# A two-image Metaformer on one core: the second expert layer of image 0 taken tile by tile between pieces of image 1's convolution and routing, and image 0's chain to its slots taken between the steps of the dense layer

## What is computed

```python
x = x + _L0_conv_ref(_ln_c(x), ...)                 # window attention, 8 heads
t = t + _L0_ffn_ref(_ln_t(t), ...)                  # 8 experts, all computed for all tokens, weighted ("dense")
x = x + _L1_conv_ref(_ln_c(x), ...)                 # 1x1 conv, group norm, 9x9 + channel conv, group norm, 1x1 conv, group norm
t = t + _L1_ffn_ref(_ln_t(t), ...)                  # 16 experts, top 2 of each token
# _L1_ffn_ref:
probs = jax.nn.softmax(logits, axis=-1)
top_probs, top_idx = jax.lax.top_k(probs, 2)
hidden = jax.nn.silu(h1) * h2
expert_out = jnp.einsum('bseh,eho->bseo', hidden, w3)
return jnp.einsum('bseo,bse->bso', expert_out, dispatch)
```

## Time and profile before

| | us |
|---|---|
| median of 3 runs | 745.42 |
| lowest and highest | 742.21, 749.3 |
| profiled execution, device time | 743.35 |
| its span (first to last instruction) | 741.5 |
| PE, POOL, ACT, DVE busy in it | 556.7, 390.7, 356.0, 353.1 |
| mean granted TensorE clock (1 is 2.4 GHz) | 0.87 |

### The profile page before, as it was taken

How to read it: one execution, slowest core, us unless ns; L and a number is a source line. 1 busy time by engine, 2 the same in 40 slices (tenths; PEclk the granted TensorE clock), 3 DMA queues, 4 the chain that set the end, 5 groups by cost and what they waited for, 6 DMA issues and landing times.

```text
span 741.5 us, 16105 instructions
## 1 busy us (share of the span) xinstructions
PE 556.7 (75%) x5352; PEld 460.7 (62%) x5353; DVE 353.1 (48%) x1021; ACT 356.0 (48%) x860; POOL 390.7 (53%) x445
## 2 busy tenths in 40 slices
PE   0567889768799998999995798452699989999000
PEld 0456677657477776677762575242699989998000
DVE  4766877756302601300117435736555545555521
ACT  1578788985573448622246241340355545555000
POOL 4667799763373986843333000675674017720773
PEclk9969999999897999999976798555699999999555
DMA  9324322211453633321940000112144334542431
GB/s 341 90 62 114 91 77 80 68 55 45 163 190 138 214 140 124 118 96 42 289 122 1 0 1 0 39 51 67 57 137 136 98 87 124 140 120 60 129 84 53
DMA packets 82188, 74.98 MB, mean 101 GB/s; under 512 B 9102, under 2 KB 74854, under 8 KB 81742
## 3 DMA queue, kind: packets, MB, share of 16 engines
q1 hardware_dynamic: 77518, 64.72, 27.3%
q0 software_dynamic: 4608, 9.45, 4.6%
HBM read 50.92 MB, written 23.63 MB: 101 GB/s over the span
## 4 chain that ended last, share of the span: by engine, by line
PE 56%; ACT 12%; DVE 12%; POOL 8%; issue 8%; DMA 3%; SPq 0%; POOLq 0%; DVEq 0%; ACTq 0%
PE bank L797 12%; PE bank L759 8%; PE bank L858 8%; PE bank L742 7%; PE bank L808 6%; POOL gathered_or_att L636 4%; ACT normed L903 3%; PE bank L719 3%; PE bank L311 3%; ACT gathered_or_att L935 2%; DVE ln_stats L1078 2%; PE bank L788 2%; PE bank L757 1%; POOL gathered_or_att L577 1%; PE bank L692 1%
## 5 line engine op out<-in xcount | busy, mean ns | idle before, releaser
L612 POOL TENSOR_TENSOR padded_or_w<-padded_or_w,gathered_or_att 128x384 f32<-128x384 f32 x96 | 95.2, 999 | 87.4 <-ACT padded_or_w L974 71.9
L624 POOL DMA_INDIRECT sorted_x<-normed,slot x72 | 71.1, 988 | 97.3 <-DVE slot L1294 76.0
L636 POOL DMA_INDIRECT gathered_or_att<-sorted_y,slot x72 | 70.2, 975 | 94.4 <-DMA sorted_y<-padded_or_w 73.1
L974 ACT ACTIVATE padded_or_w<-bank,moe_b 128x384 f32<-128x384 f32 x96 | 55.3, 580 | 99.1 <-PE bank L742 98.8
L759 PEld LDWEIGHTS bank<-moe_or_conv,padded_or_w 128*128 128x128 f32 x576 | 82.4, 201 | 31.6 <-issue 10.6
L759 PE MATMUL bank<-moe_or_conv,padded_or_w 128*128 128x128 f32 x576 | 86.1, 289 | 0.0
L742 PE MATMUL bank<-chan_major,moe_or_conv 128*128 128x384 f32 x192 | 80.5, 503 | 0.2 <-ACT padded_or_w L974 0.2
L1323 DVE TENSOR_TENSOR att_or_moe<-att_or_moe,bank 128x256 f32<-128x256 f32 x104 | 43.7, 420 | 57.8 <-PE bank L808 40.9
L988 ACT ACTIVATE att_or_moe<-bank 128x256 f32<-128x256 f32 x104 | 39.9, 383 | 61.0 <-PE bank L797 59.8
L808 PE MATMUL bank<-w,att_or_moe 128*128 x416 | 63.7, 277 | 0.6 <-ACT padded_or_w L993 0.6
L797 PE MATMUL bank<-att_or_moe,chan_major 128*128 128x128 f32 x416 | 56.7, 281 | 6.9 <-DVE chan_major L1315 6.9
(11 more groups left out here) (168 smaller groups left out, 1081.9 us busy)
## 6 DMA issues: line engine op xcount, KB each, us to landing
gathered_or_att<-combine SPq DMA_DIRECT2D x24, 768.0 KB, 4.2
padded_or_w<-windows SPq DMA_DIRECT2D x192, 48.0 KB, 1.9
sorted_x<-zeros SPq DMA_DIRECT2D x26, 256.0 KB, 3.9
padded_or_w<-sorted_x SPq DMA_DIRECT2D x26, 256.0 KB
sorted_y<-padded_or_w SPq DMA_DIRECT2D x26, 256.0 KB, 2.3
padded_or_w<-in_moe_w SPq DMA_DIRECT2D x8, 512.0 KB, 5.3
residual<-in_x_tok SPq DMA_DIRECT2D x2, 1152.0 KB, 6.2
out<-residual SPq DMA_DIRECT2D x12, 192.0 KB, 2.4
```

The source lines that it names most:

```text
L612: nc.gpsimd.tensor_tensor(HB[n % DRING], HB[n % DRING], GB_[k % 3][:, n % 4, :], ALU.mult).then_inc(S("gated"), 1)
L624: nc.gpsimd.indirect_dma_start(xs_dram[b], bass.IndirectOffsetOnAxis(ap=POS[b][:, k, t:t + 1], axis=0), TN[b][:, t, :], None).then_inc(S(f ...
L636: nc.gpsimd.indirect_dma_start(G[k][:, t, :], None, ys_dram[b], bass.IndirectOffsetOnAxis(ap=POS[b][:, k, t:t + 1], axis=0)).then_inc(S(f" ...
L974: nc.scalar.activation(HB[n % DRING], banks[HBANK[n % 2]][:, 0:DG], ACT.Gelu, bias=B1C[:, e:e + 1]).then_inc(S("gelu"), 1)
```

## The change

- The second half of the dense layer (`D` 52 to 99) carries more: the taps of image 0 come in 6 pieces of 9 and no longer in 18 of 3, and all of image 0's chain up to the third piece of its choice (`XU`, group norm, `XUH`, `XZ`, layer norm, `RT`, `LG`, `RC 0` to `RC 3`) stands between steps.
- After the dense layer come image 1's layer norm, the rest of image 0's choice, `RP 0` and `RS 0` (slots and scatter), and only then image 1's first convolution, its taps and its middle group norm.
- `M 0` is no longer a loop but 56 written-out steps (`tile_steps`), and the rest of image 1's convolution, its routing, `RP 1` and `RS 1` stand between its steps 0 to 25. `M 1` stays a loop.
- PSUM banks: `M 0` has one bank for transposes and one for results where it had two of each; `XU` of image 1 has two where it had four.
- A group norm's DVE part is cut in three pieces (`GN`, `GV`, `GF`), so that other work can stand between.

```diff
-            *every(56, 2, groups("AN", "XL", 0)), (61, ("XC", 0)), (62, ("XCE", 0)), (62, ("GN", "XC", 0)), (65, ("GS", "XC", 0)), (67, ("GQ", "XC", 0)),
-            (69, ("XCH", 0)), *every(71, 1, taps(0, 0, 54)), (89, ("GN", "XM", 0)), (91, ("GS", "XM", 0)), (93, ("GQ", "XM", 0)), (95, ("XMH", 0)),
-            *every(96, 1, [("XU", 0, n) for n in range(4)])])
-        order += [*normed("XL", 1), *[("XU", 0, n) for n in range(4, 8)], ("GN", "XU", 0), *groups("XG", 1), ("GS", "XU", 0), ("GQ", "XU", 0),
-                  ("XC", 1), ("XCE", 1), ("GN", "XC", 1), ("GS", "XC", 1), ("GQ", "XC", 1), ("XCH", 1), *groups("XUH", 0),
...
+            *every(55, 1, groups("AN", "XL", 0)), (60, ("XC", 0)), (60, ("XCE", 0)), (60, ("GN", "XC", 0)), (62, ("GS", "XC", 0)), (62, ("GV", "XC", 0)), (64, ("GQ", "XC", 0)), (64, ("GF", "XC", 0)),
+            (65, ("XCH", 0)), *every(67, 1, taps(0, 0, 54, 9)), (73, ("GN", "XM", 0)), (75, ("GS", "XM", 0)), (75, ("GV", "XM", 0)), (76, ("GQ", "XM", 0)), (76, ("GF", "XM", 0)), (77, ("XMH", 0)),
+            *every(78, 0.25, [("XU", 0, n) for n in range(8)]), (80, ("GN", "XU", 0)), (82, ("GS", "XU", 0)), (82, ("GV", "XU", 0)), (83, ("GQ", "XU", 0)), (83, ("GF", "XU", 0)),
+            *every(83, 0.5, groups("XUH", 0)), *every(84, 0.5, groups("XZ", 0)), (87, ("LN", "LR", 1, 0)), (87, ("SQ", "LR", 1, 0)), (88, ("LV", "LR", 1, 0)),
+            *every(89, 0.5, groups("LT", "LR", 1, 0)), *every(90, 0.7, groups("RT", 1, 0)), (95, ("LG", 1, 0)), (96, ("RC", 1, 0, 0)), (96, ("RE", 1, 0)),
+            *every(98, 0.5, choice(1, 0, 1, 4))])
+        order += [("LN", "XL", 1), ("SQ", "XL", 1), ("LV", "XL", 1), *groups("LT", "XL", 1), *choice(1, 0, 4, 6), ("RP", 0), *groups("AN", "XL", 1),
+                  *groups("XG", 1), ("RS", 0), ("XC", 1), ("XCE", 1), ("GN", "XC", 1), ("GS", "XC", 1), ("GV", "XC", 1), ("GQ", "XC", 1), ("GF", "XC", 1), ("XCH", 1), *taps(1, 0, 54, 9),
+                  ("GN", "XM", 1), ("GS", "XM", 1), ("GV", "XM", 1), ("GQ", "XM", 1), ("GF", "XM", 1), ("XMH", 1)]
+        order += beside("M0", 0, J + MLAG, [
+            *every(0, 0.5, [("XU", 1, n) for n in range(8)]), (3, ("GN", "XU", 1)), (6, ("GS", "XU", 1)), (6, ("GV", "XU", 1)), (6, ("GQ", "XU", 1)), (6, ("GF", "XU", 1)),
+            *every(7, 0.5, groups("XUH", 1)), *every(8, 0.5, groups("XZ", 1)), (11, ("LN", "LR", 1, 1)), (11, ("SQ", "LR", 1, 1)), (12, ("LV", "LR", 1, 1)),
+            *every(12, 0.5, groups("LT", "LR", 1, 1)), *every(13, 0.5, groups("RT", 1, 1)), (16, ("LG", 1, 1)), (17, ("RC", 1, 1, 0)), (17, ("RE", 1, 1)),
+            *every(19, 1, choice(1, 1, 1, 6)), (24, ("RP", 1)), (25, ("RS", 1))])
+        order += [("M1",), *[("F", b) for b in range(NB)]]
...
-        UP = ((6, 7), (4, 5, 3, 2))
+        UP = ((6, 7), (4, 5))
+        PREFIX = ((6, 7), (4, 5))
+        XBANK, MBANK, OBANK = ((7, 7), (0, 1)), (2, 3), ((6, 6), (6, 7))
...
+        def tile_steps(eng, b, step, experts=True):
...
+            def at(j):
+                q, r = divmod(j, RING)
...
+                step(j, r, q % 2, expert, load)
+
+            return at
...
-                tile_groups(pe, b, step, 4)
+                return tile_steps(pe, b, step) if b == 0 else tile_groups(pe, b, step, MLAG)
```

More of the change, by code:

```diff
@@ L46, in metaformer_program @@
     DLAG, DRING = 4, 5
+    MLAG = 4
     ROWS = EX[0] * TG
@@ L186, in every, with taps @@
             return [(start + int(k * step), piece) for k, piece in enumerate(pieces)]
-        def taps(b, first, last):
-            return [("XT", b, m, min(m + 3, last)) for m in range(first, last, 3)]
+        def taps(b, first, last, size=3):
+            return [("XT", b, m, min(m + size, last)) for m in range(first, last, size)]
         def normed(*ln):
@@ L340, in run, with load, expert @@
                     phases[name](*where)
+        def tile_steps(eng, b, step, experts=True):
+            words, word = EPK[b], {}
+            def at(j):
+                q, r = divmod(j, RING)
+                if r == 0:
+                    word["before"] = word.get("now")
+                def load():
+                    if experts and q < J // RING:
+                        word["now"] = eng.value_load(words[0:1, q:q + 1], min_val=0, max_val=2 ** (BITS * RING) - 1)
+                def expert(k):
+                    slot = r - k
+                    bits = word["now"] if slot >= 0 else word["before"]
+                    shift = BITS * (slot % RING)
+                    return (bits >> shift) & (EX[1] - 1) if shift else bits & (EX[1] - 1)
+                step(j, r, q % 2, expert, load)
+            return at
         def tile_groups(eng, b, step, lag, experts=True):
@@ L813, in step @@
                     ok = lambda k: not isinstance(j, int) or 0 <= j - k < J
+                    if isinstance(j, int) and j == 0:
+                        ready()
                     if ok(0):
@@ L981, in xt @@
                         act.wait_ge(S("h_full1"), j + 1 - RING + b * J)
-                    nc.scalar.activation(XTS[r][:, :], banks[r % 2][:, 0:P], ACT.Copy).then_inc(S("xt_out"), 1)
+                    nc.scalar.activation(XTS[r][:, :], banks[XBANK[b][r % 2]][:, 0:P], ACT.Copy).then_inc(S("xt_out"), 1)
                 def nonlin(j, r):
@@ L1002, in step @@
                         tail(j - 4, r, 1 - h)
-                tile_groups(act, b, step, 4, experts=False)
+                return tile_steps(act, b, step, experts=False) if b == 0 else tile_groups(act, b, step, MLAG, experts=False)
             def gn_sqrt(name, b):
@@ L1332, in step, with ready @@
                         first(j - 2, (r + 2) % RING)
-                if b == 0:
-                    dve.wait_ge(S("moe1_in"), 16 * (1 + EX[1] // 2))
-                dve.wait_ge(S(f"experts{b}"), 1)
-                tile_groups(dve, b, step, 4)
+                def ready():
+                    if b == 0:
+                        dve.wait_ge(S("moe1_in"), 16 * (1 + EX[1] // 2))
+                    dve.wait_ge(S(f"experts{b}"), 1)
+                return tile_steps(dve, b, step) if b == 0 else tile_groups(dve, b, step, MLAG)
             def combine(b):
```

80 lines of the change are left out of this document (45 added, 35 removed).

## The result

The changed kernel takes 787.7 us (median of four runs, 781.6 to 793.8) against 746.6 for the kernel before: the ratio is 1.052, with a 95% interval of 1.047 to 1.058. That is slower by 5.2%. Ratios and intervals leave out executions in which the granted clock was lower and the time longer (here the one of 793.8), so that they can differ a little from the quotient of the medians. The profiled execution took 786.2 us, with a span of 784.3.

What follows compares the result with a forecast made beforehand. The prediction saw PE idle between two busy stretches; afterwards image 1's slots (587) and scatter bound `M 1`'s start at 637.5. Adding 134.4 and 1 gave span 773, with 1.85 and 2.1 more 776 us, range 752 to 792.

Steps and rivals of the forecast that it cites:

- The hold on POOL's queue: Zeroing behind image 0's 36 scatter DMAs (46.6 us) holds image 1's taps until 472.2; without it, about 432.
- One sign of being wrong: The prediction called itself wrong if, among other signs, the dense layer ended after 406.
- The dense layer: Its second half: 12.1 us added on PE, 4.9 given back at the tail, 2.5 for stalls; end 388.5 to 398.2.
- From the logits to image 0's slots: Image 0's choice, prefix sums and slots with image 1's norm work on DVE: 27.5 us, slots at 423.
- `XU` to the slots: Image 1's chain between `M 0`'s steps: 8 + 51.5 (chain alone, from statistics) - 3.4 + 21.6 = 78 us, within 58 to 88.
- the 8 for `XU` and the first two steps: Start of image 1's chain in `M 0`, ahead of the group norm's statistics: 8 us allowed.
- My 21.6 of DVE's own work: 26 weight copies at 0.442 and 24 products at 0.42 us, in order between image 1's pieces on DVE: 21.6 us.
- The function sets: ACT's three changes of function set in `M 0`, six loads of 1.28 us: 7.7 us, counted in the upper bound of 88.
- its 784: Forecast time if each of six loads in `M 0` cost the skill's 2.66 us, drain included: 8 us more.
- The hidden chain: Rival: DVE's waits take up `M 0`'s tile work, slots 58 us behind its start and not 78; 756 us, chance 0.2.
- the taps that are not held: Rival: zeroing doesn't end the wait, image 1's taps start near 432; 741 or 731 us, chance 0.08.
- The low clock: Rival: PE stays at 1.2 GHz in `M 0`'s first half, some 4 us per step; 15 us more, 791, chance 0.12.

Runs made afterwards that it cites:

- e1: The changed kernel with POOL's zeroing of image 1's padded image moved ahead of image 0's scatter: 760.9 us, ratio 1.021 to the kernel before.
- e2: The changed kernel with image 1's whole chain from `XU` to its slots ahead of `M 0`, zeroing left in place: 799.8 us, ratio 1.069.
- e4: The changed kernel without DVE's 52 copies of an expert's weights in `M 0`, expert choice left out there: 782.9 us, ratio 1.050.
- e5: e1 with image 1's `XU` and its group norm ahead of `M 0`'s first step: 852.5 us where the kernel before took 855.0, ratio 0.999.
- e8: e6 with image 0's logits and choice behind the dense layer, and image 1's logits and first choice ahead of `M 0`: 856.0 us, kernel before 856.2.
- e9: e8 with image 1's choice and slots spread over `M 0`'s first 16 steps instead of 8: 857.1 us, kernel before 856.2.
- e12: e1 with image 1's pieces between `M 0`'s first 13 steps, not 26: 855.5 us, ratio 1.002 to the kernel before.
- e6: Against e1: image 0's choice and slots beside image 1's taps, most of image 1's chain ahead of `M 0`: 841.9 us, ratio 0.983 to the kernel before.
- e3: The changed kernel with both the zeroing ahead of image 0's scatter and image 1's whole chain ahead of `M 0`: 758.2 us, ratio 1.015.

## Why the prediction was right

Forecast 776 within 752 to 792, slower; measured 787.7. By its steps, in the time of the profiled execution:

| step | predicted | measured |
|---|---|---|
| image 0's logits done | 395.5 | 402.2 |
| dense layer's end | 398.2 | 407.4 |
| slots of image 0, scatter 0 starts | 423 | 429.8 |
| zeroing on POOL | 469.9 | 475.3 |
| taps of image 1 | 472.2, for 31.9 | 477.4, for 29.0 |
| `XU` to slots of image 1 | 78, of 58 to 88 | 84.8 |
| `M 0`'s first 26 steps | about 3 each | 508.4 to 586.8, 3.1 each |
| `M 1` starts | 637.5 | 647.8 |
| from there to the end | 135.4 | 136.5 |

- *The hold on POOL's queue* came as forecast, by row and by releaser, and e1 shows it by removing it alone. PE's wait ahead of the taps was 42.3 us, a little under the 45 to 50 that I named.
- *One sign of being wrong came true:* the dense layer ended after 406, at 407.4. The mechanism behind the forecast held even so; what the sign caught is the next term.
- *The dense layer* is one of two terms that were mis-sized: it grew by 18.8 us and not by 9.7. I gave back 4.9 us for the tail at clock 0.65. The changed kernel has such a tail too: its last 24 products take 5.32 us, where 24 of them take 3.3 at full clock. PE's busy time from 200 us to the end of the layer grew by 14.7 us (184.7 to 199.4) against my 12.1 - 4.9, its idle time by 4.1 (3.9 to 8.0) against my 2.5. Of the 6.7 us that the logits were late 5.2 were left at the taps, and 2.9 came back there, since PE ran them at clock 0.90. That I had not foreseen; it is luck that it made up for part of the miss.
- *From the logits to image 0's slots* 27.5 was forecast and 27.6 measured.
- *`XU` to the slots* was near the upper end, as taken, and 6.8 over my 78. The other mis-sized term is the 8 for `XU` and the first two steps. The group norm's statistics, with which the 51.5 begin, start 14.2 us behind `XU` (e2, without tile steps there: 8.7):

```profile
525.63 2.86 DVE L1401 BATCH_NORM_STATS2 gn_stats<-chan_major 128x6 f32<-128x384 f32 x6 [1.98 <-ACT chan_major L1086]
```

```profile
527.48 2.86 DVE L1399 BATCH_NORM_STATS2 gn_stats<-chan_major 128x6 f32<-128x384 f32 x6 [9.82 <-ACT chan_major L1084]
```

From there to the slots are 70.6 us, against 69.7 in my sum, and 51.6 in e2. So the steps cost the chain 24.5 us in all, 5.5 ahead of the statistics and 19.0 behind them; DVE's busy time is 18.0 of the 24.5 (48.9 against 31.0) and 6.5 are more waiting. My 21.6 of DVE's own work has the right size, but it doesn't add up as I said: in e4 half of it was taken away, 9.0 us up to the slots, and gave back 4.0.
- *The function sets.* Seven loads lie in the stretch and six were counted. ACT's timeline has one whole switch:

```profile
516.78 0.28 ACT L1024 ACTIVATE chan_major<-bank 128x128 f32<-128x128 f32 x1
517.07 1.28 ACT L1030 ACT_TABLE_LOAD   x1
518.49 0.38 ACT L1030 ACTIVATE att_or_moe<-bank 128x256 f32<-128x256 f32 x1
```

From the end of the one activation to the start of the next are 1.43 us; the 2.66 that the Trainium skill, page "ScalarE: Activation LUTs", section "What ACT_TABLE_LOAD costs", counts for a switch is not seen here either, and that its 784 lies nearer the measured time than my 776 is no evidence for it.
- *The rivals.* The hidden chain (58) fell with 84.8, the taps that are not held fell with 477.4. The low clock came in part:

```profile
511.40:530.30 18.90, 18.87 (x62) 13.98 (x62) 6.08 (x17) 8.19 (x20) 0.00 (x0) 0.51 0.05 15
530.30:553.00 22.70, 16.40 (x128) 14.79 (x126) 16.84 (x63) 15.86 (x38) 0.00 (x0) 0.94 0.17 48
553.00:571.00 18.00, 18.00 (x117) 17.98 (x116) 6.69 (x19) 10.04 (x30) 0.00 (x0) 0.69 0.11 30
```

PE had no idle time in the first and the last of these windows, so for 37 of the 84.8 us it, and not DVE, was the bound, against my "the stretch is not PE's". A step took 3.1 us and not the rival's 4. The 6.2 us over my 8 lie in that first window, and my estimate from its clock is that its 18.9 us would be some 9 at the full one; no run has the same pieces at full clock. Of the 11.3 us by which the span exceeds my sum (784.3 against 773), 2.3 stood at `XU`, 6.8 are the chain's and 2.2 came behind it. So the low clock is the likely main cause of the miss, and the rival's 791, which I gave 0.12, lies nearer the measured 787.7 than my 776.
- *The sum* 772.9 + 1.85 + 2.1 is 777; I wrote 776.

## What to carry to other kernels

Where a queue holds a long run of issues (36 indirect DMAs, 46 us), look for every small instruction that others wait for and that an edit has put behind it, and for every tile step whose wait for the landing has been put ahead of someone else's work: here a MEMSET of 0.77 us cost some 24 us, and one transposition, by the rows of e1, 9 us of the path. Pieces laid between tile steps pay for each step ahead of them (some 0.85 us of 1.45 here), so that interleaving gave back 10 us or nothing where it seemed to fill 42. The order that won by about 1% laid one image's choice beside the other's taps, where DVE had been idle; that this is what won is likely and not shown.

## What the runs showed of the hardware

On three of the five chips that the experiments ran on, the kernel before took some 855 us and not 747. The profiles of the others there (none was taken of the kernel before) show PE's products 2.1 to 2.8 us apart, or PE at a stand for up to 25 us, in stretches in which POOL was issuing indirect DMAs, mostly with no releaser in the trace. Five different orders (the kernel before, those of e5, e8, e9 and e12) took 852.5 to 857.1 there; only e6 was faster (841.9), which no run explains.

PE's busy time alone doesn't make its clock: 18.87 of 18.90 us busy at clock 0.51, directly behind the taps at 0.90 and a wait of 2.7 us. And the clock in the dense layer differs between profiled executions of kernels in which that layer is the same (from 360 to 400, 1.00 in the changed kernel and e1, 0.91 in e3, 0.79 in e2), with up to 7 us at the layer's end, as much as some of the edits here are worth. The four runs of e3 alone have mean clocks of 0.857 to 0.879.
